# Edge codes in half-width pieces inside the gated attention's loop, gamma loaded first, a row of ones on GpSimd, graph features without a wait

## The chip, the cores and the metric

The kernel runs on one core of one Trainium2 chip. Its engines are TensorE (PE, matmuls), VectorE (DVE), ScalarE (ACT), GpSimd (POOL) and SyncE (SP, which here issues the transfers). The metric is the time of one execution on the device, in microseconds (us), lower being better.

## The reference, cut to what matters

A two-layer network over 4 sequences of 1024 image tokens and 32 text tokens with 64 features, so N = 4224 rows. Five parts follow one another, and each but the first adds to the running h after a normalization:

```
h = gated(x); h = concat(h, txt)
h = h + attention(layernorm(h))            # 8 heads, causal, ALiBi
h = h + binary_experts(layernorm(h))
h = h + retention(layernorm(h))
h = h + graph_experts(layernorm(h), edge_index)

# gated attention
q, k, v = x @ Wq + bq, x @ Wk + bk, x @ Wv + bv
retained = (d_gamma * (q @ k.T)) @ v       # d_gamma is 1024 x 1024
y = retained @ Wo + bo; out = where(y >= 0, y, prelu_a * y)

# graph experts: M = N rows, 262144 edges plus one loop for each row
hg = (x @ W_gat).reshape(M, 4, 4)
a_src, a_dst = (hg * att_src).sum(-1), (hg * att_dst).sum(-1)
e = leaky_relu(a_src[src] + a_dst[dst], 0.2)
alpha = softmax of e over the edges of each dst
agg = segment_sum(hg[src] * alpha, dst) + b_gat
scores = mean over heads of layernorm(agg); two of four experts by top_k
out = sum over experts of gate * (gelu(x @ W1[e] + b1[e]) @ W2[e] + b2[e])
```

Edges refer to 16384 rows, of which only N exist. The kernel gives each edge a number that holds destination and source, sorts these numbers during the softmax attention and works on the few that matter in the graph part. Making the numbers ("codes") needs only `edge_index`.

## The kernel before

The parts are blocks of hand-written instruction streams, one per engine, ordered by semaphores. Between two blocks all engines meet. `norm` stands four times (r = 0 to 3) between the parts.

**Gated attention** (`gated_attention`). SP issues all loads in one queue: ident, x of the first pair of sequences, 17 small transfers, the two halves of `edge_index` (L201, L202, 1 MB each), gamma in four pieces of 1 MB (L205), x of the second pair (L207), identb. PE transposes x, makes q, k and v (`prepare`, L237, L241, L245), transposes the text (L296) and gamma (`turn_gamma`, L253), and then runs a loop of 2 pairs x 16 steps: step g has `score` (L266, two matmuls into two PSUM banks), the multiply with gamma on DVE (L431, 128x1024, PSUM times SBUF), and `weigh` (L281, two matmuls). PE issues score(n + 1) before weigh(n); score(g) waits until multiply g - 2 is done, weigh(g) for multiply g. In pair 0 PE also turns the second half of gamma (steps 0 to 7) and prepares pair 1 (steps 8 to 15); `project` (L287) and, on DVE, `finish` (L416, L420) end each half pair. ACT empties the banks of the preparation, except those of v, which DVE takes (`take_v`, L383). L296 waits for the first of these.

DVE begins with the codes: it waits for both halves of `edge_index`, then runs 16 instructions over 128x2048 (L391 to L406), each waiting for the one before it (`chain`). Only then come take_v(0, 6), take_v(0, 7) and the loop. `shi` and `dhi` use the space of the multiply's outputs, `pp`. At the end of the part SP stores `keys` and `far` (L216, L217) behind the last output.

**norm(r)**. PE transposes the additions (L483), DVE adds them to h (L501 or L503), and for r < 2 DVE sets row D of xT, one partition of 4224 columns, to 1.0 (L505). Then DVE takes mean and variance in two halves (L520 to L530) with ACT (L537, L540), PE transposes back (L491) and ACT fills xT (L544). A GpSimd body `clear` runs beside it where one is given: r = 0 has a long one (its last instruction is L741), r = 1 has none. Row D is read in the binary experts (L1303), the features (L1690) and the experts of the graph part (L2567).

**Graph experts** (`graph_experts`, `NodeTables`). After norm(3), DVE decodes the sorted codes (L1624 on), then clears row D of the feature weights (L1706, the first count of `step`), and PE's `features` (L1690, 33 matmuls with 65 rows, two records each in the profile) waits for that count. DVE's `terms` (L1710 on) waits for the features; its table is written to DRAM by `write`, and GpSimd gathers from it (L1865, 160 times) and then adds a bias (L1868). DVE makes the one-hots (L2025) meanwhile, PE counts and runs the experts, and ten groups of edges follow. The numbers in `write`, `exps` and the late wait of PE are counts of `step`.

## Time and profile before

| | us |
|---|---|
| median of 3 runs | 1418.79 (1412.3, 1418.79, 1440.24) |
| profiled execution | 1412.49 |
| its span | 1410.0 |
| mean granted TensorE clock | 0.872 |

The profile is of one execution. A row of a timeline gives start and duration in us, engine, line, operation, output and inputs, count, and in brackets how long the engine was idle before it and what released it. A row with a count stands for several instructions in a row; its duration runs from the first's start to the last's end. The granted clock is given as a share of 2.4 GHz, so 0.50 is 1.2 GHz. DMA share is the mean busy share of the 16 DMA engines.

### The profile page before, as it was taken

The numbers are of one execution on the slowest core, as the hardware profiler recorded it, in microseconds if no ns is written. First come the engines' busy times: TensorE is split into PE (matmuls) and PEld (weight loads), VectorE is DVE, ScalarE is ACT, GpSimd is POOL, SyncE is SP. The second block draws the span as 40 slices with busy tenths as digits, with TensorE's granted clock in tenths as the row PEclk, the third lists the DMA queues.
The fourth block names the chain that finished last, engine by engine and source line by source line (L and its number), as shares of the span: only waits on it lengthen the run. The fifth ranks groups of instructions, "written<-read, shape, count | busy, mean of one in ns | idle before, by whom it ended". The sixth has DMA issues, their size and how long they took to land. (4 is left out here: it accounts for less than half of the span.)

```text
span 1410.0 us, 29905 instructions
## 1 busy us (share of the span) xinstructions
PE 1122.6 (80%) x11867; PEld 648.3 (46%) x11867; DVE 985.3 (70%) x2120; ACT 460.0 (33%) x855; POOL 277.9 (20%) x312
## 2 busy tenths in 40 slices
PE   2499279999999999999938999995956989588440
PEld 1232144556555565555626333333425767577340
DVE  3645547898888889898355355554464994799977
ACT  1120144355534344343325344443111233322120
POOL 0000450010010101001003000000000577777505
PEclk9799689999999999999955899997975696799785
DMA  6000220000000000000010443402020211011001
GB/s 217 0 8 16 81 91 2 3 2 3 2 3 13 7 2 3 3 2 7 10 57 6 106 90 82 87 5 49 20 66 0 17 10 10 9 10 9 0 1 31
DMA packets 54835, 40.15 MB, mean 28 GB/s; under 512 B 27171, under 2 KB 51363, under 8 KB 53684
## 3 DMA queue, kind: packets, MB, share of 16 engines
q1 hardware_dynamic: 49588, 36.70, 10.3%
q0 software_dynamic: 5120, 1.65, 1.6%
q8 instruction: 92, 1.51, 0.4%
q14 instruction: 35, 0.29, 0.1%
HBM read 14.80 MB, written 4.94 MB: 14 GB/s over the span
## 5 line engine op out<-in xcount | busy, mean ns | idle before, releaser
L1100 DVE CUSTOM_DVE_ANT_0 ps<-ps,arena 128x512 f32<-128x512 f32 (+3 forms) x384 | 209.0, 595 | 60.1 <-PE ps L878 59.1
L1046 ACT ACTIVATE arena<-ps 128x512 f32<-128x512 f32 (+1 forms) x320 | 160.0, 552 | 211.3 <-PE ps L903 211.2
L892 PE MATMUL ps<-arena 32*128 32x256 f32 (+3 forms) x1856 | 213.9, 350 | 3.1 <-ACT arena L1046 2.3
L878 PE MATMUL ps<-arena 32*128 32x512 f32 (+3 forms) x768 | 167.4, 531 | 9.9 <-DVE arena L1100 9.4
L892 PEld LDWEIGHTS ps<-arena 32*128 32x128 f32 (+1 forms) x1856 | 138.1, 183 | 73.3 <-issue 49.7
L1865 POOL DMA_INDIRECT arena<-node_table,arena x160 | 151.9, 949 | 55.5 <-issue 48.4
L1450 DVE TENSOR_SCALAR arena<-ps 128x704 bf16<-128x704 f32 x96 | 85.6, 892 | 78.1 <-PE ps L1393 78.1
L817 POOL TENSOR_SCALAR_AFFINE_SELECT arena<-arena 128x512 f32<-128x512 f32 (+1 forms) x72 | 41.5, 597 | 459.9 <-ACT arena L1046 413.2
L925 PE MATMUL ps<-arena 128*32 128x256 f32 (+3 forms) x1856 | 110.3, 322 | 0.9 <-POOL arena L817 0.3
L929 PE MATMUL ps<-arena 128*32 128x256 f32 (+3 forms) x1856 | 106.3, 312 | 0.0
L1430 ACT ACTIVATE arena<-ps 128x704 bf16<-128x704 f32 x96 | 72.2, 757 | 97.1 <-PE ps L1393 97.1
L1406 PE MATMUL ps<-arena 128*64 128x352 bf16 x384 | 92.3, 324 | 2.8 <-DVE arena L1450 1.4
L1393 PE MATMUL ps<-arena 96*128 96x352 bf16 x384 | 89.1, 317 | 1.3 <-DMA arena<-arena 0.9
L1916 PE MATMUL ps<-arena 128*128 128x220 f32 (+6 forms) x256 | 65.9, 374 | 26.9 <-DVE arena L2108 26.6
L2025 DVE TENSOR_TENSOR arena<-arena,ps 128x4096 bf16<-128x4096 bf16 (+1 forms) x18 | 79.2, 4484 | 0.0
L1147 DVE RECIPROCAL arena<-ps 128x128 f32<-128x128 f32 (+1 forms) x72 | 63.8, 886 | 20.8 <-PE ps L929 20.5
L878 PEld LDWEIGHTS ps<-arena 32*128 32x128 f32 x768 | 55.7, 185 | 25.7 <-DVE arena L1100 19.6
L431 DVE TENSOR_TENSOR arena<-ps,arena 128x1024 f32<-128x1024 f32 x32 | 39.0, 1224 | 39.6 <-PE ps L266 39.6
L491 PE MATMUL ps<-ident,xhat 128*64 128x128 f32 x132 | 23.7, 361 | 53.5 <-DVE xhat L530 53.5
L903 PE MATMUL ps<-arena 32*128 32x256 bf16 (+3 forms) x928 | 66.0, 232 | 0.0
L929 PEld LDWEIGHTS ps<-arena 128*32 128x32 f32 (+1 forms) x1856 | 53.2, 113 | 22.3 <-issue 0.9
L1916 PEld LDWEIGHTS ps<-arena 128*128 128x128 f32 x256 | 43.7, 196 | 33.5 <-ACT arena L1974 18.3
(299 smaller groups left out, 1848.8 us busy)
## 6 DMA issues: line engine op xcount, KB each, us to landing
arena<-arena SPq DMA_DIRECT2D x144, 88.0 KB, 2.2
arena<-in_L_tok_d_gamma_batched SPq DMA_DIRECT2D x4, 1024.0 KB, 13.6
arena<-node_table,arena POOLq DMA_INDIRECT x160, 2.4
arena<-xT SPq DMA_DIRECT2D x8, 264.0 KB, 4.1
xT<-in_L_ffn_edge_index SPq DMA_DIRECT2D x2, 1024.0 KB, 7.6
dT<-arena SPq DMA_DIRECT2D x12, 88.0 KB, 2.1
arena<-in_x SPq DMA_DIRECT2D x4, 256.0 KB, 9.4
dT<-arena SPq DMA_DIRECT2D x8, 128.0 KB, 2.3
```

The costliest lines, as they stand in the source:

```text
L878: last = pe.matmul(to[:, hd % 2, at:at + wd], qu[r, P * j:P * j + P], ku[r, lo:lo + wd], start=(at == 0), stop=True, skip_group_check=True)
L892: pe.matmul(to[0:r, hd % 2, at:at + wd], ku[d, P * j:P * j + r], qu[d, lo:lo + wd], start=(at == 0), stop=False, skip_group_check=True)
L925: pe.matmul(bank[d, t0:t0 + wd], v[b][0:r, 256 * j + P * g + HD * hd:256 * j + P * g + HD * hd + HD], prob[s % NPB][0:r, hd, at:at + wd], ...
L929: last = pe.matmul(bank[d, W + t0:W + t0 + wd], ones[0:r, :], prob[s % NPB][0:r, hd, at:at + wd], start=False, stop=final, skip_group_chec ...
L1046: last = act.activation(to[:, x, 0:at + wd], src[:, x, 0:at + wd], ACT.Exp, scale=unit)
L1100: last = dve.tensor_tensor_reduce(tile, tile, distance[:, first:first + wd], 1.0, most if lo > 0 else -3e38, ALU.add, ALU.max, most)
L1393: last = pe.matmul(ps[:, 2 * (m_ % 3) + f, 0:CH], wl[:, P * (2 * n + f):P * (2 * n + f) + P], stack[q][:, n, :], start=True, stop=True)
L1406: last = pe.matmul(ps[0:D, sum_bank[q], 0:CH], pair_sum_big if on_dve[n] else pair_sum, sgn[m_ % NS][:, f, :], start=(n == 0 and f == 0), ...
L1450: dve.tensor_scalar(sgn[m_ % NS], ps[:, b0:b0 + 2, 0:CH], TINY, -TINY, ALU.min, ALU.max).then_inc(sign_dve, 1)
L1865: pool.indirect_dma_start(rows_[:, c, :], None, tab, bass.IndirectOffsetOnAxis(ap=srci[:, c:c + 1], axis=0)).then_inc(gathered[g], 16)
L1916: last = pe.matmul(ps[:, 0, CHN * lo:CHN * (lo + low)], lhs, src[:, c, 0:CHN * low], start=False, stop=False, skip_group_check=True)
L2025: last = dve.tensor_tensor(onehot[b % 2][:, :, lo:lo + width], digits[:, at:at + CB].rearrange("p (e o) -> p e o", o=1).broadcast_to([P, C ...
```

## The change

The 16 chained instructions go. Their work is done by `edge(i)`, 32 pieces of 1024 columns each, even numbers for the left half and odd ones for the right. Piece i waits until piece i - 2 is done, piece 0 for the two edge loads. The pieces are issued behind each multiply from step 2 on, as many as keep floor(32 (g - 1) / 25) issued, so that the last is behind step 26; the take_v and finish of a step come before its pieces. `shi` and `dhi` move into `keys` and `tmp`, since `pp` is in use in the loop. On SP the two edge loads go behind gamma and the second x. The memset in `norm` goes for r = 0 and r = 1, and norm(1) gets a GpSimd body that sets the row. `features` reads 64 rows instead of 65 and no longer waits for `step`; the memset of the weights' row goes, and the counts of `step` fall by one.

```diff
@@ gated_attention
-    shi, dhi = (pp[:, EC * i:EC * i + EC].bitcast(I32) for i in range(2))
+    shi, dhi = keys.bitcast(I32), tmp.bitcast(I32)
-    EDGE_STEPS = 16
+    EDGE_STEPS, EDGE_END = 32, 27
@@ SP
-            e = a["L1_ffn_edge_index"].rearrange("s (p e) -> s p e", p=P)
-            sp.dma_start(src, e[0]).then_inc(edges_in, 16)
-            sp.dma_start(dst, e[1]).then_inc(edges_in, 16)
             gsrc = a["L0_tok_d_gamma_batched"].rearrange("(k p) s -> p k s", p=P)
             for n in range(4):
                 sp.dma_start(g3[:, 2 * n:2 * n + 2, :], gsrc[:, 2 * n:2 * n + 2, :]).then_inc(gamma_in[n // 2], 16)
             for b in range(2):
                 sp.dma_start(xn[1].rearrange("p (k b d) -> p k b d", k=NB, b=2)[:, :, b, :], xsrc[2 + b]).then_inc(x_in[1], 16)
+            e = a["L1_ffn_edge_index"].rearrange("s (p e) -> s p e", p=P)
+            sp.dma_start(src, e[0]).then_inc(edges_in, 16)
+            sp.dma_start(dst, e[1]).then_inc(edges_in, 16)
@@ DVE
+            def edge(i):
+                k = slice(EC // 2 * (i % 2), EC // 2 * (i % 2) + EC // 2)
+                if i == 0:
+                    dve.wait_ge(edges_in, 32)
+                if i >= 2:
+                    dve.wait_ge(edge_step, i - 1)
+                n = i // 2
+                if n == 0:
+                    last = dve.tensor_scalar(near[:, k], src[:, k], float(N - 1), None, ALU.is_lt)
...
+                elif n == 4:
+                    last = dve.tensor_scalar(far[:, k], dhi[:, k], float(32 << 14), float(-(544 << 14)), ALU.mult, ALU.add)
+                elif n == 5:
+                    last = dve.scalar_tensor_tensor(far[:, k], shi[:, k], float((1 << 14) - P), far[:, k], ALU.mult, ALU.add)
...
+                elif n == 14:
+                    last = dve.tensor_scalar(tmp[:, k], tmp[:, k], -NONE, NONE, ALU.mult, ALU.add)
+                else:
+                    last = dve.tensor_tensor(far[:, k], far[:, k], tmp[:, k], ALU.add)
+                last.then_inc(edge_step, 1)
-            dve.wait_ge(edges_in, 32)
-            chain(dve.tensor_scalar(near, src, float(N - 1), None, ALU.is_lt))
...
-            chain(dve.tensor_tensor(far, far, tmp, ALU.add))
-            assert n == EDGE_STEPS, n
             dve.wait_ge(loaded, 16 * 17)
             for i in (6, 7):
                 take_v(0, i)
...
+            edges = 0
             for pair in range(PAIRS):
                 for n in range(STEPS):
...
                     if n == NB + 3:
                         finish(pair, 0)
+                    while g >= 2 and edges < min(EDGE_STEPS, EDGE_STEPS * (g - 1) // (EDGE_END - 2)):
+                        edge(edges)
+                        edges += 1
                 finish(pair, 1)
@@ norm
-            if r < 2:
-                dve.memset(xT[D:D + 1, :], 1.0)
@@ binary_experts
+    def ones_row(pool):
+        pool.memset(m["xT"][D:D + 1, :], 1.0)
+
-    norm(m, 1, loads)
+    norm(m, 1, loads, ones_row)
@@ NodeTables
     def write(self, sp):
-        sp.wait_ge(self.step, 7)
+        sp.wait_ge(self.step, 6)
     def features(self, pe):
         pe.wait_ge(self.loaded, 112)
-        pe.wait_ge(self.step, 1)
         for k in range(NT):
-            last = pe.matmul(ps[:, k // 32, HE * (k % 32):HE * (k % 32) + HE], xT[:, P * k:P * k + P], self.wg,
+            last = pe.matmul(ps[:, k // 32, HE * (k % 32):HE * (k % 32) + HE], xT[0:D, P * k:P * k + P], self.wg[0:D],
                              start=True, stop=True)
     def exps(self, act):
-        act.wait_ge(self.step, 15)
+        act.wait_ge(self.step, 14)
     def terms(self, dve):
-        chain(dve.memset(self.wg[D:D + 1], 0.0))
@@ graph_experts, PE
-            pe.wait_ge(tables.step, 3)
+            pe.wait_ge(tables.step, 2)
```

The kinds of the pieces, by n = i // 2: one tensor input (`tensor_scalar`) for n = 0, 1, 2, 3, 4, 10 and 14, so 14 pieces; two tensor inputs for the other nine, so 18 pieces.

## Rows read from the trace of the kernel before

**Rows 1.** The page, busy time of each engine.

```profile
PE 1122.6 (80%) x11867; PEld 648.3 (46%) x11867; DVE 985.3 (70%) x2120; ACT 460.0 (33%) x855; POOL 277.9 (20%) x312
```

**Rows 2.** Windows: stretch, length, busy and count by engine, clock, DMA, GB/s.

```profile
32.00:34.00 2.00, 0.00 (x0) 0.00 (x0) 1.97 (x2) 0.00 (x0) 0.00 (x0) 0.50 0.96 164
```

**Rows 3.** Timeline of the start, DVE and PE.

```profile
22.24 1.23 DVE L391 TENSOR_SCALAR h<-xT 128x2048 f32<-128x2048 int32 x1 [22.24 <-DMA xT<-in_L_ffn_edge_index]
...
23.59 2.05 PE L245 MATMUL ps<-weights,arena 128*128 128x128 f32 x16
...
28.54 2.29 DVE L396 SCALAR_TENSOR_TENSOR arena<-arena 128x2048 f32<-128x2048 int32 x1
...
52.00 1.29 DVE L383 TENSOR_TENSOR arena<-ps,weights 128x512 f32<-128x512 f32 x2
...
52.75 0.42 PE L296 MATMUL ps<-ident,arena 128*64 128x128 f32 x1 [27.11 <-DVE arena L383]
...
59.41 1.99 PE L266 MATMUL ps<-arena 64*128 64x512 f32 x8
```

**Rows 4.** Timeline of the loop.

```profile
75.36 1.23 DVE L431 TENSOR_TENSOR arena<-ps,arena 128x1024 f32<-128x1024 f32 x1 [1.43 <-PE ps L266]
...
105.97 1.08 PE L281 MATMUL ps<-arena 128*64 128x512 f32 x4 [1.91 <-DVE arena L431]
...
112.16 2.35 DVE L431 TENSOR_TENSOR arena<-ps,arena 128x1024 f32<-128x1024 f32 x2
...
117.78 1.23 DVE L431 TENSOR_TENSOR arena<-ps,arena 128x1024 f32<-128x1024 f32 x1 [0.84 <-PE ps L266]
```

**Rows 5.** Windows in the loop, at the turn to pair 1.

```profile
108.00:110.00 2.00, 2.00 (x5) 0.70 (x4) 0.69 (x1) 0.00 (x0) 0.00 (x0) 0.50 0.00 0
...
112.00:114.00 2.00, 1.01 (x7) 0.23 (x4) 2.00 (x3) 0.00 (x0) 0.00 (x0) 1.00 0.29 67
```

**Rows 6.** Timeline of the first norm.

```profile
163.67 3.58 DVE L505 MEMSET xT<- 1x4224 f32 x1 [0.93 <-issue]
...
167.26 1.22 DVE L520 TENSOR_REDUCE stats<-h 128x16 f32<-128x1024 f32 x1
...
168.97 4.70 POOL L738 TENSOR_SCALAR arena<-arena 128x1024 f32<-128x1024 f32 x1
...
171.72 1.29 DVE L522 TENSOR_TENSOR xhat<-h,stats 128x1088 f32<-128x1088 f32 x1
...
176.61 1.23 DVE L530 TENSOR_TENSOR xhat<-xhat,stats 128x1024 f32<-128x1024 f32 x1
177.69 2.35 POOL L741 TENSOR_TENSOR arena<-arena 128x1024 f32<-128x1024 f32 x1
...
182.40 2.35 ACT L544 ACTIVATE xT<-ps 64x512 f32<-64x512 f32 x5 [0.26 <-PE ps L491]
```

**Rows 7.** Timeline of the graph part, its first 27 us.

```profile
1063.31 0.24 DVE L1624 TENSOR_SCALAR arena<-arena 128x160 f32<-128x160 f32 x1 [4.80 <-PEq L469]
...
1074.96 14.23 PE L1690 MATMUL ps<-arena,xT 65*128 65x16 f32 x66 [12.67 <-DVE arena L1706]
...
1089.33 0.17 DVE L1710 COPY arena<-ps 128x16 f32<-128x16 f32 x1 [14.51 <-PE ps L1690]
```

**Rows 8.** Timeline of SP's queue.

```profile
13.16 0.43 SPq L201 DMA_DIRECT2D xT<-in_L_ffn_edge_index  x1
...
14.11 2.64 SPq L205 DMA_DIRECT2D arena<-in_L_tok_d_gamma_batched  x4
16.79 12.13 SPq L207 DMA_DIRECT2D arena<-in_x  x2
```

**Rows 9.** Timeline of PE behind the second norm.

```profile
740.91 12.85 PE L1303 MATMUL ps<-arena,xT 65*128 65x8 f32 x66 [1.03 <-PEq L469]
```

**Rows 10.** Timeline of DVE in the graph part.

```profile
1311.61 15.82 DVE L2084 TENSOR_TENSOR arena<-arena 128x64 f32<-128x64 f32 x1
```

**Rows 11.** Window in the graph part.

```profile
1180.00:1200.00 20.00, 19.74 (x77) 15.29 (x78) 0.00 (x0) 7.53 (x13) 15.10 (x16) 0.50 0.13 11
```

More of the change, by code:

```diff
@@ L369, in _ @@
         def _(dve):
-            n = 0
-            def chain(instruction):
-                nonlocal n
-                n += 1
-                instruction.then_inc(edge_step, 1)
-                dve.wait_ge(edge_step, n)
+            def edge(i):
[7 more added lines that the diff above has]
+                    last = dve.tensor_scalar(near[:, k], src[:, k], float(N - 1), None, ALU.is_lt)
+                elif n == 1:
+                    last = dve.tensor_scalar(src[:, k], src[:, k], float(N - 1), None, ALU.min)
+                elif n == 2:
+                    last = dve.tensor_scalar(shi[:, k], src[:, k], 7, None, ALU.arith_shift_right)
+                elif n == 3:
+                    last = dve.tensor_scalar(dhi[:, k], dst[:, k], 7, None, ALU.arith_shift_right)
+                elif n == 4:
+                    last = dve.tensor_scalar(far[:, k], dhi[:, k], float(32 << 14), float(-(544 << 14)), ALU.mult, ALU.add)
+                elif n == 5:
+                    last = dve.scalar_tensor_tensor(far[:, k], shi[:, k], float((1 << 14) - P), far[:, k], ALU.mult, ALU.add)
+                elif n == 6:
+                    last = dve.scalar_tensor_tensor(far[:, k], dst[:, k], float(P), far[:, k], ALU.mult, ALU.add)
+                elif n == 7:
+                    last = dve.tensor_tensor(far[:, k], src[:, k], far[:, k], ALU.add)
+                elif n == 8:
+                    last = dve.scalar_tensor_tensor(tmp[:, k], dst[:, k], float(N), near[:, k], ALU.is_lt, ALU.mult)
+                elif n == 9:
+                    last = dve.tensor_tensor(keys[:, k], far[:, k], tmp[:, k], ALU.mult)
+                elif n == 10:
+                    last = dve.tensor_scalar(tmp[:, k], tmp[:, k], -NONE, NONE, ALU.mult, ALU.add)
+                elif n == 11:
+                    last = dve.tensor_tensor(keys[:, k], keys[:, k], tmp[:, k], ALU.add)
+                elif n == 12:
+                    last = dve.scalar_tensor_tensor(tmp[:, k], dst[:, k], float(N), near[:, k], ALU.is_lt, ALU.is_gt)
+                elif n == 13:
+                    last = dve.tensor_tensor(far[:, k], far[:, k], tmp[:, k], ALU.mult)
+                elif n == 14:
+                    last = dve.tensor_scalar(tmp[:, k], tmp[:, k], -NONE, NONE, ALU.mult, ALU.add)
+                else:
+                    last = dve.tensor_tensor(far[:, k], far[:, k], tmp[:, k], ALU.add)
+                last.then_inc(edge_step, 1)
```

14 lines of the change are left out of this document (removed).

## The prediction

> **What bounds the kernel now.** I read the page first. No engine is full: TensorE (PE), the busiest, works 80% of the span [rows 1]. So the limit has to be read stage by stage, from windows and timelines, at the four places that the diff touches.
>
> Start of the gated attention. The window from 32 to 34 us shows VectorE (DVE) busy 1.97 of 2, every other engine empty and the granted TensorE clock at 0.50, which is 1.2 GHz [rows 2]. The timeline says why: DVE works through 16 whole-width instructions (L391 to L406) from 22.24 to 52.0, and only then takes the two V tiles (L383). PE had finished their matmuls at 25.6 (23.59 + 2.05) and sits idle 27.11 us until L296 [rows 3]. All of this is on the path.
>
> The loop of 32 steps. PE sets its period: 2.66 us in pair 0 (1.23 of DVE work and 1.43 idle) and 2.07 us in pair 1 (1.23 and 0.84 idle) [rows 4]. The idle time is where the edge work would go. After the 1.91 us in which PE waited for DVE before 105.97 [rows 4] the clock was 0.50 from 108 to 110 [rows 5].
>
> The first norm. A memset on one partition stands between the copies and the statistics: L505 shows 3.58 us after 0.93 us of "issue", and L520 starts at 167.26 [rows 6]. All 4.52 us (162.74 to 167.26) belong to it. The second norm repeats these rows at 719.60 and 723.20.
>
> The graph stage. DVE decodes edges from the block's begin at 1063.31; only behind that stands the small memset that PE waits for. PE starts the features at 1074.96, needs 14.23 us, and DVE waits 14.51 us for them until 1089.33 [rows 7].
>
> **The change, part by part.**
>
> *Edge codes moved into the loop.* Without them DVE can take V tile 6 as soon as PE has made it, about 24.7, and L296 follows at 25.7 (PE's own order) where it stood at 52.75: 27.0 us earlier. L296 to the first score took 6.66 us (59.41 - 52.75), partly at 1.2 GHz; at 2.4 GHz I give it 0.2 us less. The loop starts **27.2 us** earlier, at 32.2.
>
> *Price of the pieces.* There are 32. An instruction with two tensors took 2.29 us for 2048 columns (L396) [rows 3] and the nearest of 1024 columns 1.23 us (L431) [rows 4], 0.08 more than half. A one-tensor one took 1.23 us for 2048 columns (L391); with the same 0.08 on its half I estimate 0.70 us. So 18 x 1.23 + 14 x 0.70 = 31.9 us, where 9 x 2.29 + 7 x 1.23 = 29.2 us ran before. Back to back with nothing to wait for, DVE starts the next 0.10 us before the end: two L431 took 2.35 us, a pitch of 1.13 [rows 4]. A piece waits only for the one before the last, so pitches are 1.13 and 0.60. If each wait costs a gap of 0.03 us instead, as in the old chain, they are 1.26 and 0.73; that is the other bound.
>
> *What hides them.* The schedule floor(32(g-1)/25) puts pieces 0 to 16 behind steps 2 to 15 (one per step, two at 5, 9 and 12) and 17 to 31 behind steps 16 to 26 (two at 16, 19, 23 and 26). In pair 0 a piece of 1.13 fits the 1.43 us, and a double step eats slack that the next returns, with one exception. At step 14 DVE waits for PE in take_v, and piece 15 then stands between that and multiply 15, for which PE already waits: **+1.1 us** (bounds 1.1 to 1.3). In pair 1 the pieces are 11 with two tensors and 4 with one: 11 x 1.13 (multiplies) + 11 x 1.13 + 4 x 0.60 = 27.3 us for eleven steps in which PE needs 11 x 2.07 = 22.8. Walked from step to step, multiply 27 starts at 139.4 on the old clock instead of 135.4: **+4.0 us** (bounds 3.5, and 7.4 with the slow pitches). DVE is the bound there, and all behind it on PE and ACT waits with it.
>
> *Gamma ahead of the edges on SP.* Gamma is then issued at 13.2 and its first half can land when the edges do now, about 22; it is wanted at 26.5. x for pair 1 is wanted at step 8. The edges are now behind 4 MB of gamma and x, whose two issues alone held SP for 12.13 us [rows 8]. In the old order DMA is busy to 34, at the end with the small packets of x (0.96 at 164 GB/s) [rows 2]; the same bytes in another order end there or up to 3 us later, and the first piece, behind multiply 2, wants them near 38.8. Cost zero; cover 1 to 4 us, and then 1.4 us per step.
>
> The two DMAs of keys and far wait for piece 32 (step 26, before the last output) and stay last on SP. First stage: -27.2 + 1.1 + 4.0 = **-22.1 us**.
>
> *Memset of the ones row.* Removed in norm 0: -4.5 + 0.05 = -4.45. ACT's last L544 ends at 184.75 now and would at 180.3; POOL, which starts with the block and is unmoved, ends its own list with L741 at 180.04 [rows 6]. So the full 4.45 holds, barely; every microsecond that POOL gets slower is lost (bounds 3.3 and 4.5). In norm 1 POOL does the row: POOL is then idle for the 21.7 us from the copies to the end that norm 0 shows, and needs a few microseconds for a row that DVE does in 4.5; even at twice DVE's time it is hidden, -4.45. Both: **-8.9 us** (bounds -7.2 and -9.1).
>
> What does DVE meet on POOL when it runs 4.45 us earlier? L530 of the first half moves from 176.61 to 172.15, into L738 on POOL (168.97 to 173.67). The nearest row is L522, two SBUF inputs, at 171.72 in the middle of the same L738: 1.29 us for 1088 columns, where L431 takes 1.23 for 1024 [rows 4, 6]. I take no delay.
>
> The Trainium skill, SBUF — State Buffer, section "Who interferes with whom", speaks against this: a DVE instruction with two SBUF inputs and a GpSimd instruction that reads SBUF exclude each other, and the first keeps the ports to its end. By that rule L530 would start at 173.67, norm 0 would give 2.9 us, and the sum would be 1.5 us higher. L522 inside L738 does not bear it out here.
>
> *Features without a wait.* PE can start when the last block begins, 1063.3, 11.6 us earlier. The nearest operation is L1303: 66 such records over the same tiles, started right behind a norm, 12.85 us [rows 9], against 14.23 for L1690 [rows 7]. I take 12.85: features end at 1076.2, DVE copies them at 1076.5 instead of 1089.33: **-12.8 us** (bounds -11.6 with 14.23 us, and -14.6, where DVE is held by its own decode until 1074.7). The row count falls from 65 to 64, and no row has this matmul at 64 rows; half of 14.23, as at twice the clock throughout, stands as the low end only.
>
> The Trainium skill, TensorE: Matmul & The Clock Gate, section "LDWEIGHTS (loading the stationary operand)", has the load's time go by columns and not by rows; by it the 65th row gives nothing and the term stays -12.8, by the halved time it would be -14.6.
>
> Behind the features everything hangs on the same point: DVE's one-hots, the table write, POOL's gathers. Two later stretches, L2084 held for 15.82 us [rows 10] while POOL runs L1868, and 1180 to 1200, where DVE does nothing and PE works 19.74 us at 0.50 [rows 11], move along: in both the two partners shift by the same amount.
>
> **Sum.** Profiled execution 1412.49 (span 1410.0 plus 2.5): 1412.5 - 22.1 - 8.9 - 12.8 = 1368.7. The median of the runs shown is 1418.79, 6.3 above the profiled one and the fastest; I add 1.3 for that scatter: **1370 us**.
>
> **The rivals.**
>
> *The clock falls in pair 1* (12%). PE there waits 1.3 to 1.7 us at the double steps; 1.91 us before 105.97 came ahead of a fall [rows 4, 5]; from 112 to 114, with PE busy 1.01 of 2, it did not fall [rows 5]. At 1.2 GHz a step costs PE 4.14 us and not DVE's 2.5: eleven steps lose 18 us, the sum is 1370 + 15 = 1385.
>
> The Trainium skill, TensorE: Matmul & The Clock Gate, "HAM oscillation — how this bites in real kernels", describes such waits between bursts bringing the clock down each time; the window from 108 to 110 agrees, the one from 112 to 114 does not.
>
> *Slower than before* (2%): the same mechanism, over the whole loop. If PE stays at 1.2 GHz in it, 16 x 2.66 + 16 x 2.07 = 76 us more, 1446 us. It turns the sign once 44 us of PE's loop work run at the low level, some 18 steps. Against: the loop kept 1.00 with gaps of 1 us, and PE is then without the 27 us idle after which it had 0.50.
>
> *The pieces hide nowhere* (6%): each stands between a score and its multiply, so the whole 32 us come back: 1370 + 27 = 1397, no change by the measure. Against: 1.43 us idle in each step of pair 0.
>
> *Edges land late* (7%): 256-byte rows of x hold up SP's queue; were the edges to land at 45, DVE would stand at step 2 with all PE work behind it: +6, 1376.
>
> *More than forecast* (11%): features in 7 us, and the 20 us of PE work from 1180 at 2.4 GHz instead of 1.2: -2 and up to -10 more, 1358.
>
> **Chances.** The forecast as it stands 62%, the rivals 12, 2, 6, 7 and 11%. Range 1356 to 1391: from all low bounds to all high ones with some falls of the clock. About 2% is what a measurement of this kernel tells from no change; against 1418.79 that is 1390.4. Faster by over 2%: 62 + 7 + 11 + most of 12 = 90%; within 2%: 8%; slower: 2%.
>
> **What would show it.** Right: L296 near 25.7; first score near 32; DVE without idle in steps 16 to 26 with a period near 2.5, PE with gaps there; last loop matmul near 125; norm 0 and 1 4.4 us shorter; features starting with the last block, some 12.9 us long, with DVE waiting for them 1.8 us behind its decode. Wrong: a wait on the edge DMA at step 2, a clock of 0.50 in pair 1, POOL ending norm 0, or features that end before DVE's decode does.

## The result, and the profile after

| | us |
|---|---|
| before, median of 4 runs (lowest to highest) | 1416.17 (1412.3 to 1440.24) |
| after, median of 4 runs (lowest to highest) | 1369.13 (1355.01 to 1398.36) |
| ratio of the times, 95% interval | 0.965 (0.957 to 0.973) |
| forecast | 1370 (1356 to 1391) |
| profiled execution, before | 1412.49, span 1410.0 |
| profiled execution, after | 1398.36, span 1396.4 |

Faster by 3.5%, where 3.4% was forecast. Medians, here and below, are of all executions, while ratios and their intervals leave out those more than 1.5% above the fastest of their kernel, and the profile after is of one that is left out, so its span must not be held against the median. What sets it apart stands below, in the graph part. The stages are measured between the issues of SP that open and close them:

| stage | before | after | difference | forecast |
|---|---|---|---|---|
| first block | 158.2 | 135.3 | -22.9 | -22.1 |
| norm 0 | 26.8 | 23.8 | -3.1 | -4.45 |
| softmax attention | 529.1 | 530.9 | +1.8 | 0 |
| norm 1 and binary experts | 236.9 | 232.4 | -4.6 | -4.45 |
| norm 2 and retention | 91.4 | 91.3 | -0.1 | 0 |
| norm 3 and graph part, up to the write of `node_table` | 50.8 | 36.0 | -14.7 | -12.8 |
| from there to the DMA of the counts | 86.4 | 110.3 | +23.9 | 0 |
| from there to the end | 230.4 | 236.4 | +6.0 | 0 |

Every stage that the diff touches came within 2 us of its forecast. The profiled execution then lost 30 us in a stretch that it does not touch.

The start, in the timeline of PE after (start, duration, engine, line, operation; in brackets the idle time before and its releaser), beside [rows 3]:

```profile
24.90 0.28 PE L296 MATMUL ps<-ident,arena 128*64 128x128 f32 x1
25.85 1.09 PE L253 MATMUL ps<-ident,arena 128*128 128x128 f32 x8 [0.67 <-DVE arena L420]
30.96 1.99 PE L266 MATMUL ps<-arena 64*128 64x512 f32 x8
```

L296 stands at 24.90 (25.7 forecast), the first score at 30.96 instead of 59.41: 28.45 us earlier.

The loop. First the pieces on DVE in pair 1, then PE at step 14 and behind it:

```profile
92.14 0.68 DVE L403 TENSOR_SCALAR xhat<-xhat 128x1024 f32<-128x1024 f32 x1
92.74 1.22 DVE L448 TENSOR_TENSOR arena<-ps,arena 128x1024 f32<-128x1024 f32 x1
99.01 1.22 DVE L407 SCALAR_TENSOR_TENSOR xhat<-xT,h 128x1024 f32<-128x1024 int32 x1
100.14 1.22 DVE L448 TENSOR_TENSOR arena<-ps,arena 128x1024 f32<-128x1024 f32 x1
101.28 1.22 DVE L407 SCALAR_TENSOR_TENSOR xhat<-xT,h 128x1024 f32<-128x1024 int32 x1
```
```profile
78.64 1.92 PE L281 MATMUL ps<-arena 128*64 128x512 f32 x4 [3.05 <-DVE arena L448]
80.49 1.94 PE L245 MATMUL ps<-weights,arena 128*128 128x128 f32 x8
86.70 1.08 PE L281 MATMUL ps<-arena 128*64 128x512 f32 x4 [1.49 <-DVE arena L448]
90.01 1.08 PE L281 MATMUL ps<-arena 128*64 128x512 f32 x4 [1.17 <-DVE arena L448]
96.88 1.08 PE L281 MATMUL ps<-arena 128*64 128x512 f32 x4 [0.40 <-DVE arena L448]
107.17 1.08 PE L281 MATMUL ps<-arena 128*64 128x512 f32 x4 [1.36 <-DVE arena L448]
```

The L448 are the multiplies (L431 before). A piece with two tensors and a multiply start 1.13 us apart, one with one tensor takes 0.68 us and the next starts after 0.60, as worked out. From 84.73 to 116 us DVE has no idle time. PE's waits of 1.17, 0.40 and 1.36 us come behind the steps with two pieces (16, 19 and 23); the one of 1.49 was 0.98 before. Ahead of multiply 15 PE waits 3.05 us instead of the 1.91 before 105.97 in [rows 4]: the 1.1 us forecast for step 14. Behind that wait four matmuls take 1.92 us instead of 1.08, half the clock; before, those four still took 1.08, and the low clock came over the two of L287 behind them (1.91 us instead of 1.02). Through pair 1 the four take 1.08.

Norm 0 on DVE and on POOL, beside [rows 6], and then the row of ones in norm 1. The first fence is of before, the others of after:

```profile
168.51 0.38 DVE L521 TENSOR_SCALAR stats<-stats 128x16 f32<-128x16 f32 x1
174.30 0.45 DVE L526 TENSOR_SCALAR stats<-stats 128x16 f32<-128x16 f32 x1
178.17 3.03 DVE L530 TENSOR_TENSOR xhat<-xhat,stats 128x1088 f32<-128x1088 f32 x1
```
```profile
141.13 0.18 DVE L539 TENSOR_SCALAR stats<-stats 128x16 f32<-128x16 f32 x1
143.93 1.00 DVE L539 TENSOR_SCALAR stats<-stats 128x17 f32<-128x17 f32 x1
144.96 1.29 DVE L540 TENSOR_TENSOR xhat<-h,stats 128x1088 f32<-128x1088 f32 x1
147.54 0.80 DVE L544 TENSOR_SCALAR stats<-stats 128x16 f32<-128x16 f32 x1
150.19 1.23 DVE L548 TENSOR_TENSOR xhat<-xhat,stats 128x1024 f32<-128x1024 f32 x1
```
```profile
143.91 0.99 POOL L751 IOTA arena<- 128x1024 int32 x1 [0.28 <-POOL arena L786]
144.96 2.18 POOL L753 CAST arena<-arena 128x1024 f32<-128x1024 int32 x1
147.25 3.69 POOL L756 TENSOR_SCALAR arena<-arena 128x1024 f32<-128x1024 f32 x1
```
```profile
689.96 3.61 POOL L1290 MEMSET xT<- 1x4224 f32 x1 [13.33 <-POOLq L791]
```

Two of DVE's instructions on 16 or 17 columns take 1.00 and 0.80 us instead of 0.18, 1.44 us too much. Before, two of them took 0.38 and 0.45, so 0.48 us of that was there already: from the first reduction to the first L548 (L530 before) it is 10.32 us instead of 9.35, 0.97 more. The copies end and the statistics begin 4.50 us earlier in the block, and 4.50 - 0.97 = 3.53. The rest down to 3.06 is PE's 33 transposes behind L548, which took 6.60 us instead of 6.15; the clock was 0.50 until their last 2 us. In norm 1 POOL's memset of the row is over at 693.57, 2.2 us before the first of DVE's short ones; these take 0.17 or 0.18, and the whole 4.5 us arrive.

POOL's own list became longer, too: it ends 22.81 us behind the block's begin, and 21.85 before. Its conversion took 2.18 us instead of 1.04 and its second scaling 3.60 instead of 2.79, while the first, 4.70 before, took 3.69.

The features: PE's timeline, DVE's first copy of them, and PE's own records in windows of 2 us (PE busy, weight loads, granted clock, DMA share, GB/s), beside [rows 7, 9]:

```profile
1034.53 11.17 PE L1710 MATMUL ps<-arena,xT 64*128 64x16 f32 x66 [1.02 <-PEq L489]
1045.81 0.17 DVE L1729 COPY arena<-ps 128x16 f32<-128x16 f32 x1
```
```profile
1036.00:1038.00 2.00, 2.00 (x20) 2.00 (x19) 0.97 0.00 0
1038.00:1040.00 2.00, 2.00 (x12) 2.00 (x11) 0.50 0.00 0
1040.00:1042.00 2.00, 2.00 (x11) 2.00 (x11) 0.50 0.00 0
```

They start behind the last norm with the clock still high, 20 in 2 us, and go on at 11 in 2 us once it is 0.50. DVE copies them with no wait: its own decode ends at the same time.

Last, the stretch that nothing was forecast for, on DVE after (L2044, L2025 before, makes the one-hots of one count):

```profile
1085.71 8.89 DVE L2044 TENSOR_TENSOR arena<-arena,ps 128x4096 bf16<-128x4096 bf16 x2 [0.35 <-PE ps L1897]
1098.05 8.89 DVE L2044 TENSOR_TENSOR arena<-arena,ps 128x4096 bf16<-128x4096 bf16 x2 [3.45 <-PE ps L1897]
1159.71 0.27 DVE L2134 COPY arena<-ps 128x66 f32<-128x66 f32 x1 [9.26 <-PE ps L1897]
1185.26 0.31 DVE L2090 TENSOR_TENSOR arena<-ps,arena 128x144 f32<-128x144 f32 x1 [25.27 <-PE ps L1921]
```

and the same in windows of PE, DVE, ACT and POOL (clock, DMA share and GB/s at the end), after and before:

```profile
1050.00:1180.00 130.00, 127.11 (x921) 100.08 (x920) 86.13 (x36) 28.75 (x52) 93.47 (x99) 0.50 0.13 12
```
```profile
1093.62 79.24 DVE L2025 TENSOR_TENSOR arena<-arena,ps 128x4096 bf16<-128x4096 bf16 x18
1100.00:1190.00 90.00, 81.26 (x875) 62.13 (x876) 79.12 (x33) 26.28 (x48) 67.38 (x71) 0.78 0.11 10
```

Before, DVE made all 18 one-hots in 79.24 us without a wait, and PE kept up at a mean clock of 0.78. After, PE had 0.50 throughout, needed 12.3 us for a chunk of products and its count, and DVE waited 3.45 us for each.

### The profile page after: what moved, and what is told of

Its sections match the earlier page's. It is cut to its first block and busy times, and to the rows that moved or that the text cites. A ratio compares the mean times of both kernels' runs of the same rounds, so it can differ in the third digit from the quotient of the medians.

```text
span 1396.4 us, 29918 instructions
## 1 busy us (share of the span) xinstructions
PE 1156.2 (83%) x11867; PEld 675.8 (48%) x11867; DVE 976.9 (70%) x2133; ACT 460.0 (33%) x855; POOL 282.8 (20%) x313
## 5 line engine op out<-in xcount | busy, mean ns | idle before, releaser
L943 PE MATMUL ps<-arena 128*32 128x256 f32 (+3 forms) x1856 | 110.3, 322 | 0.9 <-POOL arena L835 0.3
L2044 DVE TENSOR_TENSOR arena<-arena,ps 128x4096 bf16<-128x4096 bf16 (+1 forms) x18 | 79.7, 4481 | 14.1 <-PE ps L1897 14.1
L1935 PE MATMUL ps<-arena 128*128 128x220 f32 (+6 forms) x256 | 66.2, 374 | 27.4 <-DVE arena L2127 27.2
L1165 DVE RECIPROCAL arena<-ps 128x128 f32<-128x128 f32 (+1 forms) x72 | 63.8, 886 | 21.1 <-PE ps L947 20.8
L2594 PEld LDWEIGHTS ps<-weights 128*128 128x128 f32 x264 | 61.8, 334 | 13.3 <-issue 13.3
L2586 PE MATMUL ps<-xT,weights 65*128 65x384 f32 x88 | 63.8, 880 | 0.0
```

The source lines that it names most:

```text
L943: pe.matmul(bank[d, t0:t0 + wd], v[b][0:r, 256 * j + P * g + HD * hd:256 * j + P * g + HD * hd + HD], prob[s % NPB][0:r, hd, at:at + wd], ...
L2044: last = dve.tensor_tensor(onehot[b % 2][:, :, lo:lo + width], digits[:, at:at + CB].rearrange("p (e o) -> p e o", o=1).broadcast_to([P, C ...
```

## The experiments

All kernels of one group ran on the same chip with runs of the kernel before between them. Medians, with the ratio to before and its 95% interval where there is one:

| kernel | median (lowest to highest), us | ratio | first block / norm 0 / write to counts / rest, us |
|---|---|---|---|
| whole change again | 1375.18 (1361.5 to 1380.59) | 0.967 (0.958 to 0.976) | 135.4 / 23.3 / 105.2 / 224.7 |
| loop only | 1411.47 (1392.34 to 1422.71) | 0.985 (0.976 to 0.994) | 135.2 / 27.3 / 110.3 / 236.7 |
| norms only | 1410.93 (1400.31 to 1435.09) | none | 157.4 / 23.3 / 93.9 / 222.3 |
| features only | 1405.45 (1395.72 to 1434.73) | 0.989 (0.979 to 0.998) | 157.8 / 26.5 / 110.3 / 236.8 |
| spread schedule | 1356.80 (1345.13 to 1376.94) | 0.952 (0.944 to 0.961) | 130.8 / 23.7 / 86.8 / 229.1 |
| extra matmuls | 1357.65 (1356.18 to 1363.57) | 0.960 (0.953 to 0.967) | 137.2 / 23.3 / 86.4 / 216.9 |
| no table | 1366.81 (1350.37 to 1407.61) | 0.960 (0.952 to 0.968) | 135.4 / 21.8 / 110.3 / 237.6 |
| edges first | 1372.92 (1356.3 to 1392.56) | 0.963 (0.953 to 0.973) | 138.0 / 23.3 / 101.0 / 227.6 |
| spread + extra | 1351.85 (1341.92 to 1355.47) | 0.956 (0.947 to 0.964) | 130.6 / 23.6 / 86.4 / 218.0 |
| the same, table first | 1348.76 (1343.23 to 1352.78) | 0.956 (0.948 to 0.964) | 130.7 / 24.1 / 86.3 / 217.0 |
| first burst only | 1366.85 (1360.27 to 1375.03) | 0.970 (0.962 to 0.979) | 134.8 / 23.6 / 86.8 / 218.4 |
| whole change, third time | 1364.50 (1354.59 to 1374.36) | 0.965 (0.954 to 0.975) | 135.4 / 23.3 / 93.9 / 223.3 |

The kernel before beside them had medians of 1419.62 (first four), 1416.28 (next four) and 1415.54 (last four). By the measure of 2%, loop only and features only are unclear; norms only has no ratio.

### The whole, and each part by itself

The first is the changed kernel unchanged. The others take one part of the diff each: only the pieces and gamma's place; only the two edits of the row of ones; only the features:

```diff
 # norms only, against the kernel before
-            if r < 2:
-                dve.memset(xT[D:D + 1, :], 1.0)
-    norm(m, 1, loads)
+    norm(m, 1, loads, ones_row)
 # features only, against the kernel before
-        pe.wait_ge(self.step, 1)
-            last = pe.matmul(..., xT[:, P * k:P * k + P], self.wg,
+            last = pe.matmul(..., xT[0:D, P * k:P * k + P], self.wg[0:D],
-        chain(dve.memset(self.wg[D:D + 1], 0.0))
```

> The whole change once more, for a second profile. Theory A (the gains come from three separate places and add up; what differed between the first profile of the changed kernel and its other runs is the granted clock in the graph part): the stretch up to the first norm is again 22.9 us shorter than before (block ends at 135.3 instead of 158.2), norm 0 3.0 us, norm 1 4.5 us, and from the last norm's begin to the write of the node table 14.7 us. Sum 45 us, so 1412.5 - 45 = 1367, if the stretch behind the table write takes the 316.8 us that it took before. Rival B (features without a wait make PE start the graph part at the low clock and stay there): the stretch behind the table write is again 20 to 30 us longer than before, total 1390 to 1400.

> Only the pieces in the loop and the new order of loads; both memsets and the wait of the features as before. Theory A: the first norm begins at 135.3 instead of 158.2, everything else keeps its length, total 1412.5 - 22.9 = 1389.6. Rival B (the parts help each other: an earlier loop end moves nothing else, yet the low clock in the graph part comes from the features): graph part as before, 367.6 us. Rival C (the gain of the loop part is given back, by a lower clock in the softmax attention for instance): less than 20 us in all.

> Only the memset of the row of ones: out of norm 0, on GpSimd in norm 1. Theory A: norm 0 takes 23.8 us as in the changed kernel instead of 26.8, for DVE meets GpSimd's table instructions 4.5 us earlier and loses 1.4 us to them; norm 1 22.2 instead of 26.8. Total 1412.5 - 7.5 = 1405.0. Rival B: the 1.4 us lost in norm 0 were chance in one execution; norm 0 takes 22.4, total 1403.6. The forecast had 4.45 for each.

> Only the features: 64 rows, no wait for DVE, no memset of the weights' row. Theory A: features start with the block and take 11.2 us (the first 3 us at the high clock, the rest at the low one); the node table is written 14.7 us earlier, the part behind it takes 316.8 us as before when the clock rises again on the way; total 1412.5 - 14.7 = 1397.8. Rival B: the clock stays at 0.50 up to the edge groups whenever the features start early, the part behind the table write is 20 to 30 us longer, and the total is 1405 to 1415, no gain or a loss.

By stage the parts are separate and add up: the pieces take 23.0 us off the first block and nothing else; the norms 3.6 us off norm 0 (26.8 to 23.3) and leave the first block alone; the features 11.6 us off the way to the table (50.8 to 39.2). In total time they do not show as cleanly: the medians fall by 8.2, 8.7 and 14.2 us, 31 together, and the whole in the same company by 44.4; by the ratios, loop only and features only fall by 21 and 16 us and the whole by 47. The stage behind the table write says why single medians are blunt here: it took 110.3 us in loop only, which has the old features with their old wait, and in features only, but 93.9 in norms only. So the 110.3 of the profile after is not what starting the features early does. That was the rival I had to exclude.

Norm 0 ended in two ways. In the profile after, SP's first issue of the next block comes 0.26 us behind ACT's last L562. In the second profile of the whole change and in norms only it comes 0.47 us behind the last of POOL's list, which ends 22.8 us behind the block's begin, when ACT has been done for 0.7 and 0.5 us: PE's transposes took 5.26 and 5.39 us there. So POOL ended the norm in these two, and in the third profile of the whole change, extra matmuls and edges first; 23.25 to 23.28 us is what its list allows.

### Another schedule of the pieces

```diff
-    EDGE_STEPS, EDGE_END = 32, 27
+    EDGE_STEPS = 32
+    EDGE_BY = [0, 0, 2, 4, 6, 8, 10, 11, 12, 13, 14, 15, 16, 17, 17, 17] + list(range(18, 33)) + [32]
-                    while g >= 2 and edges < min(EDGE_STEPS, EDGE_STEPS * (g - 1) // (EDGE_END - 2)):
+                    while edges < EDGE_BY[g]:
```

> The changed kernel with another schedule of its 32 pieces: two one-tensor pieces in each of steps 2 to 6, one piece in each of steps 7 to 13, none at 14 and 15, one in each of steps 16 to 30 (before: 17 pieces up to step 15, 15 in steps 16 to 26). Theory (in pair 1 VectorE is the bound only because 15 pieces stand in eleven steps, and at step 14 a piece stands ahead of a multiply that TensorE wants): 16 multiplies, 11 two-tensor pieces at 1.13 and 4 one-tensor pieces at 0.60 are 32.9 us, where TensorE's 16 steps of 2.07 are 33.1, so the work fits; the 4.0 us of pair 1 fall to about 0.7 and the 1.1 us of step 14 vanish. The first block ends at 131 us (135.3 in the changed kernel), 1369 becomes 1365. Rival (the rest of pair 1's loss is something else, for example a half clock in its first steps): the first block ends at 134 to 136. Second rival: two pieces in steps 2 to 6 do not fit in 2.66 us (1.13 + 2 x 0.63 = 2.39) and the start of the loop slips by 1 to 2 us: 132 to 133.

The first block ends at 130.8 us although the first score stands 0.85 us later than after (31.81): from first score to the end of the block 98.97 us instead of 104.34, and 98.78 before, where the loop had no pieces at all. Windows of pair 1 (PE, weight loads, DVE, ACT, POOL, clock, DMA share, GB/s), the changed kernel and then this one:

```profile
96.00:104.00 8.00, 7.22 (x30) 1.69 (x28) 8.00 (x8) 0.00 (x0) 0.00 (x0) 1.00 0.00 0
104.00:112.00 8.00, 6.64 (x26) 1.62 (x22) 8.00 (x9) 1.18 (x2) 0.00 (x0) 1.00 0.01 2
```
```profile
96.00:104.00 8.00, 7.96 (x34) 1.93 (x32) 8.00 (x8) 0.60 (x1) 0.00 (x0) 1.00 0.01 2
104.00:112.00 8.00, 7.94 (x30) 1.88 (x30) 7.97 (x10) 0.69 (x1) 0.00 (x0) 1.00 0.15 33
```

PE is full again, where DVE alone was. The forecast's 1.1 + 4.0 = 5.1 us were a matter of where the pieces stand, not of their work, and 5.4 came back. The median is 8 us under the 1365 expected; no changed kernel ran beside this one, so the 5.4 us are shown by the stage and not by the medians.

### The order on SP's queue

```diff
+            e = a["L1_ffn_edge_index"].rearrange("s (p e) -> s p e", p=P)
+            sp.dma_start(src, e[0]).then_inc(edges_in, 16)
+            sp.dma_start(dst, e[1]).then_inc(edges_in, 16)
             gsrc = a["L0_tok_d_gamma_batched"].rearrange("(k p) s -> p k s", p=P)
```

(and the three lines gone from their place behind x).

> The changed kernel with the two edge loads back ahead of gamma on SyncE's queue, as in the kernel before. Theory (the order is worth little: the DMA has the same bytes): gamma then comes about 1 us later, its first half is wanted when the first V tiles are done; the first score stands at 31 to 32 us (30.96 in the changed kernel) and the first block ends at 135.3 to 136.5. Rival (gamma would be late by the whole time of the edge loads and the new order is what lets the loop start early): first score at 36 us or later, with TensorE waiting for SyncE's gamma at its gates, and the first block ends at 140. Either way the first piece does not wait for its edges.

```profile
27.70 1.06 PE L253 MATMUL ps<-ident,arena 128*128 128x128 f32 x8 [1.66 <-DMA arena<-in_L_tok_d_gamma_batched]
32.78 1.99 PE L266 MATMUL ps<-arena 64*128 64x512 f32 x8
```

PE waits for gamma, 1.66 us where it waited 0.67 for DVE, and the first score comes at 32.78, 1.8 us later than after, of which 0.8 was there at L296 already (25.74 against 24.90). So the order is worth 1 us, and it is not what lets the loop start. The first piece waited for its edges in neither order. The block's end at 138.0 us is beyond the 136.5 of the theory, and short of the rival's 140: besides the 1.8 us at the first score, 0.9 us lie behind the wait for multiply 15, where the low clock also took in L287 (1.92 us, 1.02 after) and the next scores (2.35 us, 1.99 after).

### Norm 0 without GpSimd's table, and with it at the head

The first kernel puts six memsets in the place of the table, the second moves `fill_table` behind the memset of `kB`:

```diff
-        fill_table(chain, pool, distance, 8 * P, 7 * P)
+        for t in (distance, *[cols[:, 7:8]] * 5):
+            chain(pool.memset(t, 0.0))
```
```diff
         chain(pool.memset(kB, 0.0))
+        fill_table(chain, pool, distance, 8 * P, 7 * P)
         for t in (*mcw, *mtw):
```

> The changed kernel without the table that GpSimd fills during norm 0 (iota, conversion, two scalings, iota, sum): six memsets stand in its place, so the causal mask and the bias of the softmax attention are wrong and the work behind them is otherwise the same. Theory (norm 0 kept only 3.05 of the 4.45 us because VectorE's short one-tensor instructions and its multiply are held by GpSimd's table work): norm 0 takes 22.2 us as norm 1 does (23.8 in the changed kernel), VectorE's instruction that took 1.00 us takes 0.18. Rival (norm 0 ends with GpSimd's own list or with ScalarE's copies whatever VectorE does, or the first norm's matmuls run at the lower clock): 23.3 to 23.8 us still. Elsewhere nothing moves.

> As the kernel with both, and GpSimd fills its table at the head of norm 0 instead of at its end, behind the two memsets that SyncE waits for: then its instructions that read run while VectorE copies from PSUM, and plain memsets run beside VectorE's short instructions. Theory (only the instructions of the table hold VectorE's short ones): norm 0 takes 22.8 us, where GpSimd's list ends, instead of 23.3 to 23.7; total 0.5 to 0.9 us less than with both. Rival (memsets hold them too, or the copies are held instead): norm 0 stays at 23.3 or more.

Without the table norm 0 takes 21.8 us, 0.4 under the theory's 22.2. This kernel has no long list on POOL either, so it takes away both what held DVE and what ended the norm. One short instruction is still long, and it ends with a plain memset of POOL (x6 is this memset, 0.95 us, and five of one column):

```profile
144.04 0.73 DVE L539 TENSOR_SCALAR stats<-stats 128x17 f32<-128x17 f32 x1
143.79 1.74 POOL L788 MEMSET arena<- 128x1024 f32 x6
```

Half of my theory falls with this row, which was to take 0.18 us: it is not only POOL's instructions that read. With the table at the head, the short ones are held by other parts of it, longer than before, and one ends when POOL's sum does:

```profile
142.86 1.57 DVE L545 TENSOR_SCALAR stats<-stats 128x16 f32<-128x16 f32 x1
142.05 2.35 POOL L760 TENSOR_TENSOR arena<-arena 128x1024 f32<-128x1024 f32 x1
```

Norm 0 takes 24.1 us, with POOL's list done after 20.8, and 23.6 in the kernel without the move: moving the work within the norm gained nothing (the 3 us between the medians of this kernel and the one without the move are inside their scatter). Taking it out of the norm gained 1.5 to 2 us.

### The clock of the graph part

```diff
             for i in range(NXC):
                 products(pe, i)
+                if i == 0:
+                    pe.wait_ge(tables.step, 2)
+                stay_warm(pe, m, 0, 16 if i == 0 else 4)
                 if i < NB:
                     count(i)
             pe.wait_ge(zeroed, 1)
-            pe.wait_ge(tables.step, 2)
```

`stay_warm` (there already, used in the binary experts) writes n results of a bf16 matmul with 512 columns into a bank that nobody reads. There are 11 chunks, so 56 extra matmuls in all, and not the 60 of the expectation. One further kernel has both this and the spread schedule, another has the first burst alone, with 0 in the place of 4.

> The changed kernel with extra bf16 matmuls of 512 columns on TensorE in the graph stage, into a PSUM bank that is free there: 16 before the first count and 4 before each later one (60 in all, results not used). Theory (the stretch from table write to the counts' DMA takes 86 to 110 us from one execution to the next only because TensorE's granted clock stays at 0.50 or rises; at 0.50 TensorE needs 12.3 us a chunk, at 1.00 VectorE is the bound with 9.6 to 10 us a count): the granted clock is 1.00 within about 15 us of the burst, the stretch takes 80 to 86 us, span and time fall by 15 to 30 us against the changed kernel, 1340 to 1355. Rival (GpSimd's 80 gathers or something else ends the stage anyway, and VectorE just waits longer behind it): the stretch becomes 86 and the wait of VectorE for the gathers grows by as much as is won, beyond 20.9 us; total within 5 us of the changed kernel. Second rival (extra matmuls do not raise the clock): they cost 60 x 0.43 = 26 us at 0.50, 1395.

> The changed kernel with both the spread schedule of the pieces (first block 130.8 us, counted from the first score 5.3 us shorter) and the extra matmuls of the graph stage (table write to the counts' DMA 86.4, what follows 216.9). If the two are independent: first block 131, span 1350 to 1352 in a profile like the others, median 1357.65 - 4.8 = 1353. Rival (the extra matmuls won nothing of their own, and low times come from executions in which the clock rises anyway): the median is that of the spread schedule alone, 1357, with the same scatter of 30 us between runs.

> The changed kernel with only the first 16 extra matmuls of the graph stage, none before the later counts. Theory A (the burst lifts the clock and the stage's own work then keeps it): clock 1.00 to the last count, the same 86 us and about the same 1357 us as with all 60. Theory B (the stage's own work lets the clock fall again, as it did for a time in the kernel before after it had risen): stretches at 0.50 come back among the later chunks, the stretch takes 90 to 105 us, 1362 to 1370, with a larger scatter.

> The changed kernel once more, beside the three above on the same chip, so that they can be compared with it: 1369 us, first block 135.4, norm 0 23.3 to 23.8, the stretch from table write to the counts' DMA anywhere between 86 and 110 us. Theory that its scatter is the clock of the graph stage: highest minus lowest time is 20 us or more here, and under 15 us for the kernels with the extra matmuls. Rival (the scatter is elsewhere): it is alike in all four.

With all extra matmuls, the one-hots of DVE, its later wait, and two windows:

```profile
1053.13 79.24 DVE L2046 TENSOR_TENSOR arena<-arena,ps 128x4096 bf16<-128x4096 bf16 x18
DVE arena L2092 <- PE ps L1921: 14.9, 4, 11.2
1055.00:1065.00 10.00, 10.00 (x100) 6.80 (x99) 10.00 (x3) 1.30 (x2) 3.26 (x4) 0.68 0.46 24
1065.00:1075.00 10.00, 9.88 (x106) 6.61 (x106) 10.00 (x3) 3.75 (x7) 7.56 (x9) 1.00 0.11 10
```

The clock is 1.00 from 1065 to 1145. DVE makes its one-hots without a wait, and the wait that was to grow by the rival fell, from 25.3 us (20.9 before) to 11.2: PE gets to its look-ups earlier, and GpSimd's gathers are not what DVE stands behind. From the table write to the end 303.3 us, after 346.7, before 316.8. The median of 1357.65 is 2.7 us above the 1340 to 1355 expected. The burst alone:

```profile
1075.00:1090.00 15.00, 12.67 (x167) 10.12 (x168) 15.00 (x5) 5.07 (x10) 11.35 (x13) 0.94 0.10 9
1090.00:1105.00 15.00, 15.00 (x129) 11.52 (x126) 15.00 (x4) 3.00 (x6) 11.34 (x13) 0.50 0.10 9
1105.00:1120.00 15.00, 14.97 (x117) 11.67 (x115) 14.64 (x5) 4.02 (x9) 11.34 (x13) 0.65 0.10 9
```

The clock rises and falls again, and the median is 1366.85, that of the changed kernel beside it (1364.50). This profile, of the fastest of its four executions, still took 86.8 us for the stretch (90 to 105 were expected with a falling clock) and 305.2 from the table write to the end, 2 us more than with all extra matmuls. So what the slower three lost is not traced; by the medians the burst by itself gained nothing measurable.

What the stretch takes goes with the moment at which the clock rises. The first window of 10 us, counted from the table write, with a mean clock above 0.6:

| kernels | window, us | stretch, us |
|---|---|---|
| extra matmuls, spread + extra, the same with table first | 10 to 20 | 86.3 to 86.4 |
| before | 20 to 30 | 86.4 |
| spread schedule | 30 to 40 | 86.8 |
| norms only; whole change, third time | 60 to 70 | 93.9 |
| edges first | 80 to 90 | 101.0 |
| whole change again | 90 to 100 | 105.2 |
| after, loop only, features only, no table | none | 110.3 |

DVE's next wait, for PE's look-ups, goes with the clock as well: 25.3 us after and 20.9 before, where the clock at the head of the rest is 0.50; 15.4, 14.9, 11.6 and 10.8 in whole change again, edges first, whole change for the third time and norms only, where it is 1.00. With the burst alone it rose from 10 to 20 us, was back at 0.50 from 40 to 60, and the stretch took 86.8. What decides when the clock rises, in kernels with the same instructions in this stretch, no run shows.

The scatter: lowest to highest is 7, 14 and 10 us in the three kernels with all extra matmuls, and 43, 19, 20 and 32 us in the three runs of the changed kernel and in the spread schedule alone; but it is 15 us with the burst alone, where more was expected, and the third whole change, with 19.8, misses the 20 expected of it by a little. Across the profiles the stretch took 86 to 110 us without them and 86.3 or 86.4 with all of them. That fits the theory; it is shown for the profiles and only inferred for the times. Not all of the scatter lies there: the softmax attention took 527 to 537 us from profile to profile, which no run here explains.

The kernel with spread schedule and extra matmuls has 1351.85, 12.7 us below the changed kernel beside it (5.4 of which the pieces' stage accounts for), and with the table first 1348.76: both are 0.956 of the kernel before. Against the changed kernel's 0.965 the intervals overlap.

## Why the prediction was right, and where it was lucky

**Start of the loop.** Forecast -27.2, measured -28.45. L296 was 0.8 us earlier than thought, of which 0.6 is the start of the launch itself: L245 begins at 22.97 and not at 23.59, which says nothing of the change (it is 25.05 in the kernel with extra matmuls). From L296 to the first score 6.06 us instead of the 6.46 that I gave (6.66 less 0.2). Right, 1.25 us short.

**Pieces.** Forecast +5.1 for step 14 and pair 1. From the first score to the last `project` it was 87.3 us before and 92.85 after: +5.55, of which 1.14 is the wait for multiply 15, 4.09 is pair 1 and 0.3 the low clock between them. Pitches, the place and size of the wait at step 14, and the places of PE's waits came as worked out, and the spread schedule, which removes just these two, gave 5.4 back. Of the two bounds for a piece the cheap one held: a wait on a piece two places back costs nothing.

**Gamma and edges.** Cost zero, cover 1 to 4 us: no wait on the edges; the order itself is worth 1 us in favour of the change, which I had not counted.

**Norm 0.** The term was -4.45 with 3.3 as its low bound, and 3.06 was measured (3.6 in the two other profiles of the whole change and in norms only). Two steps failed. The first is "What does DVE meet on POOL when it runs 4.45 us earlier?". I looked at the first L530, which indeed ran beside POOL unheld (L548 now, 1.23 us), and not at the short instructions between, which met POOL's iota and scaling and cost 0.97 us more than before. The trace of before had such rows: L521 with 0.38 us ends within 0.02 us of POOL's conversion, L526 with 0.45 within 0.02 us of POOL's second iota, and the second L530, with two SBUF inputs, took 3.03 us instead of 1.29 (3.03 and 3.02 in loop only and features only as well), ending 1.16 us behind POOL's L741. So the rule that L522 did not bear out is borne out by this row beside it. The second step is POOL "unmoved", ending its list at 180.04: it met DVE elsewhere and ended 0.96 us later in the block, which left no room under 23.25 us; in five profiles it is what ended the norm, the sign that I had named. The Trainium skill, SBUF — State Buffer, section "Who interferes with whom", which I had weighed only for instructions with two SBUF inputs, also says that `tensor_scalar` can enter a mode that takes the ports shared with GpSimd, and that the one that comes second blocks. Three rows here agree: those of 0.73, 1.00 and 1.57 us end within 0.03 us of the POOL instruction beside them. Those of 0.80 us and of 0.92 us (table first) do not; they ended in the middle of POOL's scaling.

**Norm 1.** -4.45 forecast, -4.6 measured. Two numbers of the recorded working are loose, and neither enters the sum: POOL's free time, given as 21.7 us, is 22.0 from the end of the copies to ACT's last L544, and the bound of -7.2 for both norms does not follow from 3.3 and 4.45, which give -7.75.

**Features.** -12.8 forecast, between -11.6 and -14.6. Both ends occurred. The stage became 14.7 us shorter in four profiles (the one above, the second of the whole change, spread schedule, extra matmuls), where 66 matmuls took 11.1 or 11.2 us and DVE did not wait, and 14.0 shorter in a fifth (table first, 10.5 us). It became 11.6 shorter in six others (among them the third of the whole change and features only), where they took 13.2 or 13.3 and DVE waited 1.9 to 2.0, against 12.85 and 1.8 in the forecast. One more microsecond of those six belongs to norm 3's own transposes: 6.2 to 6.3 us instead of 5.3, by the same clock, so the step itself gave 12.6 there. What I had not seen is that the clock at the end of norm 3 decides between the two. The 65th row costs nothing: at 0.50 there are 11 matmuls in 2 us with 64 rows, and 11 with 65 (1077 to 1083 before). The Trainium skill, TensorE: Matmul & The Clock Gate, section "LDWEIGHTS (loading the stationary operand)", says the same, and these windows agree.

**"Move along".** I took the rest of the graph part as moved and not changed: "in both the two partners shift by the same amount". That step was wrong as a statement about one execution. PE's clock there is 0.50 or 1.00 for long stretches, from one execution to the next, and 24 + 6 us hang on it, more than on any part of the change. The other stretch named there, L2084 held for 15.82 us, moved along as 16.6 us after and 16.7 in the third whole change, but the longest of these ten was 12.5 us with extra matmuls and 0.26 in norms only. The medians differ by 47.0 us where 43.8 was worked out from the profile; that they agree so well is in part luck, since the medians of the parts (31 us together) do not. The profiled execution of before was a good one in this stretch (86.4 us, where 86.3 is the lowest value seen), though not behind it (230.4, where 216.9 was seen); that of after among the worst (110.3, a value that loop only, features only and no table show too). Of the rivals, none happened as a whole: no fall of the clock in pair 1, no wait on the edges, no loop that hides nothing. A part of "More than forecast" did: PE's work ahead of the look-ups at 1.00 instead of 0.50, with 11.6 us of DVE's wait instead of 20.9 in the third whole change, and features that end by the time DVE's decode does.

## What to carry to other kernels

Work moved into a loop's idle time is free only where its pieces stand at the steps that have the time; a multiply and a two-tensor piece, 2.26 us, hide under a period of 2.66 but not under one of 2.07, so count it step by step and give the shorter steps fewer pieces. When two profiles differ in a stretch that the diff does not touch, look at the granted clock there before explaining it, and compare with a run that has only another part of the change. An engine moved earlier by a removed step meets other work of its neighbours: look at all its instructions there, the short ones too, and at what the neighbour's own list then takes.

## What the runs showed of the hardware

- A `tensor_scalar` on 16 or 17 columns takes 0.17 us on DVE alone and up to 1.57 beside POOL's conversion (0.38), iota (0.45, 1.00), wide memset (0.73), scaling (0.80, 0.92) or sum (1.57); one on 17 columns ran in 0.17 beside a POOL scaling (149.69 in the changed kernel), so not every such meeting holds it.
- A DVE instruction with two SBUF inputs, 128x1088, took 3.03 us begun inside POOL's sum, and 1.29 without it; others began inside a POOL scaling and took their 1.23 or 1.29 us.
- POOL's conversion of 1024 columns took 2.18 us, begun together with a DVE instruction with two SBUF inputs, and 1.04 without one.
- A memset of one partition by 4224 columns takes 3.61 us on POOL, and took 3.58 on DVE with 0.93 us of issue ahead of it [rows 6]: no slower on POOL.
- PE, busy 127 of 130 us, had a granted clock of 0.50 from 1050 to 1180 after; with 56 bf16 matmuls among the same work it had 0.96 over 1055 to 1145. The stretch took 86.3 or 86.4 us in all three profiles with this extra work, and 86.4 to 110.3 without any.
